# A two-layer attention and expert kernel: inputs laid out by kernel(), a new order on every engine, and 27 matmuls that nothing reads

## What is computed

```python
x = x + _L0_xattn_ref(ctx_2048, _layernorm(x), mask_BxS2_ik0, L0_xattn_b)
x = x + _L0_ffn_ref(_layernorm(x), k0, k1, k2, s0, s1, s2)
x = x + _L1_xattn_ref(_layernorm(x), ctx_2048, mask_BxS2_if0, W_in, b_in, g_res, g_init)
x = x + _L1_ffn_ref(_layernorm(x), W, b, Wg, bg)
```

## Time and profile before

| | us |
|---|---|
| median of three runs | 539.66 (539.65 to 540.94) |
| the profiled execution | 538.97 |
| span of its trace | 537.2 |
| TensorE busy | 497.7 |
| DVE busy | 433.1 |
| POOL busy | 364.5 |
| ACT busy | 356.7 |

### The profile page before, as it was taken

One profiled execution on the slowest core, in us unless ns is written; L12 is line 12 of the kernel. 1 busy time (PEld: TensorE's weight loads), 2 busy tenths in 40 slices (PEclk: granted clock), 3 DMA queues, 4 the chain that ended last, 5 costly groups with the idle time before them and its releaser, 6 DMA issues.

```text
span 537.2 us, 15110 instructions
## 1 busy us (share of the span) xinstructions
PE 497.7 (93%) x5549; PEld 324.0 (60%) x5549; DVE 433.1 (81%) x1404; ACT 356.7 (66%) x761; POOL 364.5 (68%) x633
## 2 busy tenths in 40 slices
PE   1756999999999999999999999999999999999893
PEld 1645565666656565766666566666666666655551
DVE  4735868899897979888897979799887785867897
ACT  3398698887967867677686866777566665655410
POOL 7644444588858869686868778686845857654865
PEclk9987899999999999999999999999999999999997
DMA  7402101010310101010110101000000000100010
GB/s 170 101 4 55 32 16 56 2 51 6 82 36 18 34 22 51 23 50 21 31 43 21 52 1 51 21 21 27 3 21 1 2 22 1 33 1 21 1 31 29
DMA packets 28503, 16.98 MB, mean 32 GB/s; under 512 B 3687, under 2 KB 28429, under 8 KB 28430
## 3 DMA queue, kind: packets, MB, share of 16 engines
q1 hardware_dynamic: 26670, 15.57, 10.5%
q10 hardware_dynamic: 1760, 0.46, 0.4%
HBM read 11.74 MB, written 4.24 MB: 30 GB/s over the span
## 4 chain that ended last, share of the span: by engine, by line
PE 64%; DVE 5%; issue 1%; ACT 0%; DVEq 0%
PE ps L2186 16%; PE ps L2134 16%; PE ps L2145 4%; PE ps L2079 4%; PE ps L2022 4%; PE ps L2096 4%; PE ps L2127 4%; PE ps L2164 2%; PE ps L2165 2%; PE ps L2104 2%; PE ps L2054 2%; PE ps L2177 2%; DVE weighed L1046 1%; PE ps L2083 1%; PE ps L2047 1%
## 5 line engine op out<-in xcount | busy, mean ns | idle before, releaser
L2186 PE MATMUL ps<-w_moeT,y4T 128*128 128x512 f32 x256 | 123.5, 607 | 1.2 <-DVE gd L1005 1.1
L613 POOL TENSOR_TENSOR sum<-weighed 128x512 f32<-128x512 f32 x60 | 76.1, 1269 | 71.2 <-DVE weighed L1046 71.2
L2134 PE MATMUL ps<-h,w 128*128 128x512 f16 x512 | 118.6, 379 | 0.0
L1638 ACT ACTIVATE h<-ps 128x512 f16<-128x512 f32 x128 | 74.1, 591 | 46.9 <-PE ps L2134 35.9
L1046 DVE TENSOR_TENSOR weighed<-ps,wgt 128x1024 f32<-128x1024 f32 x64 | 77.8, 1218 | 31.7 <-PE ps L2186 30.7
L969 DVE SCALAR_TENSOR_TENSOR h<-ps,h 128x512 f16<-128x512 f32 x128 | 85.6, 682 | 20.2 <-ACT h L1638 20.1
L2134 PEld LDWEIGHTS ps<-h,w 128*128 128x128 f16 x512 | 48.3, 98 | 56.2 <-issue 5.6
L1604 ACT ACTIVATE prT<-ps,maskT 77x1024 f32<-77x1024 f32 x64 | 67.3, 1101 | 14.8 <-PE ps L2083 14.5
L2186 PEld LDWEIGHTS ps<-w_moeT,y4T 128*128 128x128 f32 x256 | 45.1, 189 | 43.0 <-issue 35.0
L565 POOL TENSOR_TENSOR rs<-ve,neg_half 128x4 f32<-128x4 f32 x64 | 64.9, 1013 | 8.7
L560 POOL TENSOR_TENSOR ve<-mv,eps 128x4 f32<-128x4 f32 x64 | 14.2, 222 | 60.6 <-DVE mv L903 60.4
(11 more groups left out here) (171 smaller groups left out, 986.1 us busy)
## 6 DMA issues: line engine op xcount, KB each, us to landing
cx<-in_ctx SPq DMA_DIRECT2D x16, 308.0 KB
xa<-in_x SPq DMA_DIRECT2D x16, 256.0 KB, 3.0
out_x<-xo SPq DMA_DIRECT2D x16, 256.0 KB, 2.3
plugs<-plug_d SPq DMA_DIRECT2D x16, 77.0 KB
nat<-in_L_ffn_W SPq DMA_DIRECT2D x1, 512.0 KB
k_u<-in_L_ffn_k ACTq DMA_DIRECT2D x1, 256.0 KB, 3.9
...
```

The source lines that it names most:

```text
L613: nc.gpsimd.tensor_tensor(sum4[:], both[:, 0:4 * D], both[:, 4 * D:8 * D], ALU.add).then_inc(c_sum4.sem, 1)
L1638: last = nc.scalar.activation(h[:, 0, (k - 1) % FC, :], src, ACT.Relu)
L2134: last = pe.matmul(pb(g, k), w2[:, i, c * 128:(c + 1) * 128], h1[:, g.p, part, i, :], start=(i == 0 and part == 0), stop=(i == FC - 1 and ...
L2186: last = pe.matmul(pm(g, j)[:, half, :], y4T[:, g.p, j * S:(j + 1) * S], w_moeT[:, half * 512:(half + 1) * 512], start=True, stop=True)
```

## The change

1. `laid_out()` in `kernel()` makes arrays in the order in which the tiles want them: x and the result by group as [128, 512] rows, the context as [77, 1024] rows, the keys already transposed in the form of `kT` with their zeros, the values in the form of `vx` with zeros and ones, the expert weights, W_in and the gate's transposed in one array (with a second array that repeats its last row), the signs in one array, the three scales in one, the mask turned.
2. With that, `a_turn_keys`, `a_keys`, `a_values_in`, `turn_mask`, `turn_weights`, `take_weights` and `make_head_scale` go. There are three loads for each group in place of `load_keys`: `load_context` (four buffers), `load_keys` and `load_values` (two buffers each, 308 KB each). The subtraction of the last row and the product with the gains are POOL's (`make_sums_zero`), on the turned weights.
3. The f16 weights of stage b are made on DVE (`make_weights`) and not on ACT. `a_normalise` of groups 1, 2 and 3 is on DVE.
4. In the last two groups the sums go other ways: POOL, as before, for (14,0), (14,2) and (15,0); `e_accumulate` on DVE for (14,1), (14,3), (15,2) and (15,3), eight multiply-adds of 128x128 straight from PSUM; for (15,1) ACT weighs in eight pieces, TensorE sums them with the identity (`e_sum`) and ACT copies the sum. Half of c's normalisation of group 15 is on DVE (`c_normalise_rest`).
5. Every engine's list of calls is new. The 17 `keep_busy` matmuls of the end are gone; 27 stand at seven places of the first attention, and they read `ones_bf`.

```diff
-                sp.dma_start(cx[:, g.f], ctx[g.n * G:(g.n + 1) * G].rearrange("j k d -> k j d")).then_inc(keys_in[g.f].sem, 16)
+                if g.has(2):
+                    sp.wait_ge(a_less[1].sem, a_less[1].of(g, back=2))
+                sp.dma_start(kT[:, g.p], keys[g.n]).then_inc(keys_in[g.p].sem, 16)
+
+            def load_values(g):
+
+                if g.has(2):
+                    sp.wait_ge(a_pv.sem, a_pv.of(g, back=2))
+                sp.dma_start(vx[:, g.p], values[g.n]).then_inc(values_in[g.p].sem, 16)
...
-            def a_values_in(g):
...
+            def make_weights():
+                dve.wait_ge(made_s, 6)
+                dve.wait_ge(made_halves, 1)
+                nc.vector.tensor_scalar(w1[:], k0_d[:], s_sgn[:, 7:8], None, ALU.mult)
+                nc.vector.tensor_scalar(w2[:], k1_u[:], s_sgn[:, 5:6], s_sgn[:, 6:7], ALU.mult, ALU.add)
+                nc.vector.tensor_scalar(w3[:], k2_u[:], 2.0, -1.0, ALU.mult, ALU.add).then_inc(made_ffn, 1)
...
+                for e in range(4 * half, 4 * half + 4):
+                    so_far = xo if e else xd
+                    if e:
+                        dve.wait_ge(v_step.sem, v_steps(g, j) + e)
+                    last = nc.vector.scalar_tensor_tensor(xo[:, g.p, cols], pm(g, j)[:, e // 4, (e % 4) * D:(e % 4 + 1) * D],
+                                                          wgt[:, g.p, j, e:e + 1], so_far[:, g.p, cols], ALU.mult, ALU.add)
...
-            a_turn_keys(g[0])
+            keep_busy(10, 4)
             turn_ends()
+            keep_busy(3, 4)
             a_turn_rows(g[0])
+            keep_busy(3, 4)
             a_scores(g[0], 0)
-            count_ends((s_ends, g[0]))
+            keep_busy(2, 4)
+            a_turn_rows(g[1])
+            keep_busy(3, 4)
             a_scores(g[0], 1, (a_max[0], g[0]))
```

More of the change, by code:

```diff
@@ new lines, in count, with place, place_free @@
+        def count(kind, g, j):
+            return sum(1 for i, k in sums_of if how(i)[k] in kind and (i.n, k) <= (g.n, j))
+        def place(g, j):
+            return buffered.index((g.n, j)) % 2
+        def place_free(g, j):
+            n, k = buffered[buffered.index((g.n, j)) - 2]
+            if how(Group(n))[k] == "scalar":
+                return s_sum.sem, s_sum.of(Group(n), k + 1)
+            return c_sum4.sem, added(Group(n), k)
+        def added(g, j):
+            return count(("gpsimd",), g, j)
@@ L908, in a_stats, with a_normalise @@
                 stats(ln_a, g, xa[:, g.f, :])
+            def a_normalise(g):
+                dve.wait_ge(ln_a.rs.sem, ln_a.rs.of(g))
+                if g.has(2):
+                    dve.wait_ge(a_xT.sem, a_xT.of(g, back=2))
+                for j in range(G):
+                    last = nc.vector.tensor_scalar(xn[0][:, g.p, j * D:(j + 1) * D], xa[:, g.f, j * D:(j + 1) * D],
+                                                   mv[0][:, g.p, j, 0:1], rs[0][:, g.p, j:j + 1], ALU.subtract, ALU.mult)
+                last.then_inc(a_xn_v.sem, 1)
             def a_highest(g, q):
@@ new lines, in normalise_rest @@
+            def normalise_rest(ln, g, src):
+                n, p = ln.n, g.p
+                dve.wait_ge(ln.rs.sem, ln.rs.of(g))
+                dve.wait_ge(ln.turned.sem, ln.turned_at(g, back=2))
+                for j in range(2, G):
+                    last = nc.vector.tensor_scalar(xn[n][:, p, j * D:(j + 1) * D], src[:, j * D:(j + 1) * D],
+                                                   mv[n][:, p, j, 0:1], rs[n][:, p, j:j + 1], ALU.subtract, ALU.mult)
+                last.then_inc(ln_rest[n].sem, 1)
@@ L1134, in _ @@
             b_low(g[2], 0)
+            a_stats(g[6])
             c_stats(g[1])
@@ new lines, in _ @@
+            b_high(g[6], 2)
+            a_out_copy(g[7])
+            c_normalise(g[5])
+            b_high(g[6], 3)
+            c_turned(g[5])
+            b_high(g[6], 4)
+            a_queries(g[9])
+            a_maxima(g[8])
+            a_decays(g[7])
+            b_high(g[6], 5)
+            a_normalise(g[10])
+            b_high(g[6], 6)
+            d_normalise(g[5])
+            d_turned(g[5])
+            b_high(g[6], 7)
+            b_high(g[6], 8)
+            b_normalise(g[7])
+            d_gate_exp(g[5])
@@ new lines, in _ @@
+            d_turned(g[6])
+            a_normalise(g[11])
+            b_high(g[7], 7)
+            b_high(g[7], 8)
+            d_gate_exp(g[6])
+            b_normalise(g[8])
+            a_exponent(g[9], 0)
+            b_high(g[8], 0)
+            a_exponent(g[9], 1)
+            b_high(g[8], 1)
+            b_high(g[8], 2)
+            a_out_copy(g[9])
+            c_normalise(g[7])
+            b_high(g[8], 3)
+            c_turned(g[7])
+            b_high(g[8], 4)
+            a_queries(g[11])
```

1456 lines of the change are left out of this document (781 added, 675 removed).

## The result

| | before | after |
|---|---|---|
| median | 540.3 us (539.65 to 540.96) | 549.31 us (547.94 to 549.49) |
| ratio | | 1.016, 95% interval 1.014 to 1.019 |
| span of the trace | 537.2 us | 547.4 us |
| b_last(g0) starts | 72.49 us | 84.04 us |
| from there to b_last(g15) | 427.7 us | 427.8 us |

The change makes the kernel 1.6% slower; 3.6% faster was predicted. The lower half of the table cuts the span at two starts of b_last. Against the prediction, 19.5 us are missing in the start (a lead of 8 was expected, 11.5 were lost), 6 in the middle, 3.6 in the end: the 29 us between the 519.9 of its sum and the 549.3 of the profiled execution. (Of the 6.8 us predicted for the end, 1.7 for the experts behind b_last(g15) fall into the middle of this table.)

The account below looks back on a forecast made before the run. TensorE's instructions were taken to bound the middle, chains through other engines the start and end. 538.97 - 8 (start) - 4.3 (middle) - 6.8 (end) = 519.9, 520.6 on the median; forecast 520.5 us, range 514.5 to 529.

Parts of the forecast that it names:

- a lead of 8: Start: TensorE's full stretch, from 62.67 us before, begins 8 us earlier, range 4 to 10.
- 6.8 us predicted for the end: End, after b_last(g15): sums redistributed over DVE, ACT and POOL, one expert call moved behind; 6.8 us saved, range 4 to 8.
- The 60 us of start moved 74 GB/s: Start: loads priced by bytes at 231 GB/s; 1.67 MB take 7.2 us, first scores at about 12 us.
- The first rival: Start keeps its length: DVE becomes the bound, TensorE's idle time brings slow stretches; lead 3 us, total about 525.5; 20%.
- Done at 18.5: Start, split of the maxima on DVE: four steps take 0.9 us, done at 18.5, 4.7 us earlier; 3 if the clock stays low.
- three normalisations (0.8 us each): Start: DVE takes over three normalisations at 0.8 us each, besides weights of about 3.2 us.
- The third rival: Middle: keys come late, issued from SP's queue behind its other waits; twelve groups 2 us late each, total 544.5; 4%.
- some 4: Middle, key loads: issue and landing of 308 KB take some 4 us of 11.5 us slack.
- The fourth rival: Start: TensorE stays at the low clock until 26 us whatever runs; lead about 5, total 523.5; chance counted within the forecast's 60%.
- 0.2 for 0.36: Middle: four key transposes gone, 0.36 us per group; 4.3 us over twelve groups, bound 3.8.
- a worse one can lose as much; I take nothing: Middle, order of calls: a better order finds 1.9 us at most, a worse one loses as much; counted as nothing.
- 0.28 us, so 2.3 us (bounds 1.8 and 3.2): End: eight DVE multiply-adds of 128x128 per sequence at 0.28 us each, 2.3 us in place of 3.5.

Follow-up runs that it names:

- e1_whole: Changed kernel with biases written by the host into row 127, so the weights come in one load of 128 rows; 534.83 us, 0.989 of before.
- e3_all: e1_whole plus new DVE order, more unread matmuls in start and end, two picks moved, last two DVE sums interleaved; 528.73 us, 0.981 of before.

## Why the prediction was wrong

- **Loads.** "The 60 us of start moved 74 GB/s in the mean with a DMA share of 0.32, so 231 GB/s at a full share": the step that failed. It priced every load by its bytes, only as far as the keys of group 0 (first scores at about 12; 13.1 in after, 12.4 in e1_whole), and SP's list behind them not at all. The wait for the rows of group 2, put at nothing, was 14.1 us for DVE and 18.5 for TensorE. The forms of the loads had changed and no row of before was of the new one; 127 rows ran at 26 GB/s. With the load in another form 14.5 of the 29 us are gone.
- **The start.** The first rival (20%, lead 3 us) was right in kind: DVE is the bound behind values(g0), TensorE idles 3.2 us, and the slow stretch follows. What was held against it, "most of what the chain loses is the key turn, its copy and matmuls at half clock, and these go", did not come true: the half clock stayed in part. "Done at 18.5" for the split was 21.1 (the prediction's own price for a clock that has not risen gives 20.2): the first highest started at 14.98 and not at 13.6, behind DVE's other work, and the second scores ran at the lower level. The "three normalisations (0.8 us each)" had no row and were 1.56, 2.13 and 1.12 us, in the row of DVE that was the bound; the weights were 2.2 for 3.2. With the full level in most of the start the lead is 2.4 to 5.9, not 9.
- **The third rival**, slower by keys late behind SP's waits, had the right side and the right engine and the wrong place: SP's queue, but in the first 44 us and by a load's form; TensorE waits for no load after b_last(g0). Its "some 4" for issue and landing of 308 KB was 3.2 (median of the key loads in e1_whole). The 2.7 cited beside it from the Trainium skill ("DMA: Bandwidth & Descriptors", section "Anatomy of one DMA", an estimate) is stated there for DMAs issued from GpSimd; these go out from SP.
- **The 27 matmuls.** The fourth rival is wrong as put: enough of them raise the level before 26 us. Three and two of them did not fill 2.4 and 1.0 us, and in the changed kernel itself the first scores took 1.26 us, behind a wait of 3.6 us for the rows of the mask. What the 27 were worth is not shown: 534.83 with and 535.55 without them overlap.
- **Middle.** The size per period, 0.2 for 0.36, and "a worse one can lose as much; I take nothing": it lost 2.5 to 4.5 us at two places, more than the 1.9 of that bound.
- **End.** "0.28 us, so 2.3 us (bounds 1.8 and 3.2)" was 3.04, inside the bounds and far from the value taken; and the walk to the weights was 2.1 us short, with POOL's 0.58 in it. "Before it was 32.4" should be 32.2 by the earlier trace rows (500.18 + 1.95 to 534.33); the 6.8 goes by that.
- **Range.** 514.5 to 529 held neither the result nor the kernel with the load mended, 534.8; it does hold e3_all, 528.7, but that is another kernel, with the wrong terms mended, and speaks for nothing in the forecast. The chance of 4% for slower was given to one mechanism, though each new load form was unmeasured.
